# Three substitution groups with two rows a step, the outputs' norm on ScalarE, and a read result added by two engines

## What is computed

```python
h = tokens(x)                                   # 64 x 37 x 256
h = h + attention0(layernorm(h))                # 16 heads, shared keys and values
h = h + ffn0(layernorm(h))                      # entmax router, two factored layers
h = h + attn1(layernorm(h))
h = h + ffn1(layernorm(h))                      # 8 experts, the best one for each token

# attn1, for each image and each of 2 heads (d = 128), C = one chunk of up to 64 positions:
k = x / norm(x);  beta = sigmoid(x @ W_beta.T);  v = (x @ W_write.T) * beta
A0 = tril(-((k * beta) @ k.T) * L, -1)          # L: powers of the decay
A  = solve_triangular(eye - A0, eye)            # an inverse of a 37 x 37 unit triangle
o  = (tril(k @ k.T * L)) @ (A @ v)
out = x + o @ W_read.T
```

## Time and profile before

| | |
|---|---|
| median of 3 runs | 834.07 us (833.72 to 834.9) |
| the profiled execution | 836.92 us, span 835.1 us |
| mean granted clock of TensorE | 0.886 |
| PE busy | 678.3 us (81% of the span), 4562 matmuls |
| DVE busy | 448.1 us (54%), 1266 instructions |
| ACT busy | 229.1 us (27%) |
| POOL busy | 260.3 us (31%) |

### The profile page before, as it was taken

One profiled execution on the slowest core, in us unless ns is written; L12 is line 12 of the kernel. 1 busy time (PEld: TensorE's weight loads), 2 busy tenths in 40 slices (PEclk: granted clock), 3 DMA queues, 4 the chain that ended last, 5 costly groups with the idle time before them and its releaser, 6 DMA issues. The chain is left out here.

```text
span 835.1 us, 13690 instructions
## 1 busy us (share of the span) xinstructions
PE 678.3 (81%) x4562; PEld 519.5 (62%) x4562; DVE 448.1 (54%) x1266; ACT 229.1 (27%) x635; POOL 260.3 (31%) x418
## 2 busy tenths in 40 slices
PE   5899999999977149999983385196569999999994
PEld 4567677777755139999972364085436767667673
DVE  1567777777765742444799199466613333333321
ACT  0223333333322043443431022032013232232321
POOL 2344444444441012455453122022012221222211
PEclk9899999999986558999997589578569999999998
DMA  8211111111000000000100670193411111111110
GB/s 303 93 35 34 34 35 34 34 35 33 2 2 1 0 2 0 7 7 6 25 7 4 171 303 1 27 356 96 196 50 39 57 47 50 57 44 52 51 32 20
DMA packets 24643, 49.77 MB, mean 60 GB/s; under 512 B 15284, under 2 KB 15414, under 8 KB 23936
## 3 DMA queue, kind: packets, MB, share of 16 engines
q1 hardware_dynamic: 20960, 34.43, 12.7%
q0 software_dynamic: 3328, 10.23, 4.0%
q10 hardware_dynamic: 288, 4.25, 1.3%
HBM read 39.03 MB, written 9.86 MB: 59 GB/s over the span
## 5 line engine op out<-in xcount | busy, mean ns | idle before, releaser
L1762 PE MATMUL psum<-arena_w,work 128*128 x208 | 95.9, 605 | 1.0 <-DVE work L1814 1.0
L1860 ACT ACTIVATE work<-psum,cst 128x128 f32<-128x128 f32 x208 | 56.6, 383 | 144.1 <-PE psum L1775 144.1
L1786 PE MATMUL psum<-arena_w,work 128*128 x416 | 94.2, 379 | 0.4 <-ACT work L1860 0.4
L1786 PEld LDWEIGHTS psum<-arena_w,work 128*128 128x128 f32 x416 | 77.1, 190 | 10.5 <-issue 1.1
L1724 POOL DMA_INDIRECT out<-work,row_i x26 | 25.8, 990 | 160.2 <-DVE work L1836 160.2
L1823 DVE COPY work<-psum 128x512 f32<-128x512 f32 x52 | 36.0, 692 | 70.0 <-PE psum L1762 61.9
L346 PE MATMUL psum<-arena_w 128*111 128x256 f32 x264 | 64.1, 396 | 4.9 <-DMA arena_w<-in_pack 4.9
L1762 PEld LDWEIGHTS psum<-arena_w,work 128*128 128x128 f32 x208 | 38.3, 194 | 40.1 <-issue 40.1
L711 POOL TENSOR_TENSOR arena_w<-arena_w,work 101x592 f32<-101x592 f32 x33 | 39.6, 1200 | 72.2 <-DVE work L577 72.2
L346 PEld LDWEIGHTS psum<-arena_w 128*111 128x111 f32 x264 | 46.5, 183 | 19.7 <-issue 9.6
L1130 PE MATMUL psum<-tokens,work 111*111 111x128 f32 x88 | 18.2, 340 | 43.4 <-POOL work L1537 43.4
(11 more groups left out here) (216 smaller groups left out, 1344.6 us busy)
## 6 DMA issues: line engine op xcount, KB each, us to landing
arena_w<-in_w SPq DMA_DIRECT2D x2, 4096.0 KB, 13.3
arena_w<-in_x SPq DMA_DIRECT2D x22, 333.0 KB, 2.9
x_rows<-tokens SPq DMA_DIRECT2D x22, 192.0 KB, 5.7
arena_w<-in_pack ACTq DMA_DIRECT2D x1, 2420.0 KB, 10.9
cst<-in_packc ACTq DMA_DIRECT2D x1, 1727.0 KB, 14.9
arena_w<-in_pack SPq DMA_DIRECT2D x1, 818.5 KB, 7.3
arena_w<-in_pack SPq DMA_DIRECT2D x2, 384.0 KB, 4.6
work<-a_rows SPq DMA_DIRECT2D x21, 32.4 KB, 2.0
```

Of the source, the lines that this page charges most:

```text
L1762: mm = nc.tensor.matmul(bank[2 * j + f][:, :], xgt[j][:, k * 128:(k + 1) * 128], arena_w1[:, bass.ds(expert * (2 * FF) + (k * FF + f * 512 ...
L1786: mm = nc.tensor.matmul(bank[7][:, 0:D], ht[j][:, g * 128:(g + 1) * 128], arena_w2[:, bass.ds(expert * (FC * D) + g * D, D)], start=(g == ...
L1860: nc.scalar.activation(ht[j][:, g * 128:(g + 1) * 128], bank[4 + f][:, k * 128:(k + 1) * 128], ACT.Gelu, bias=cst[:, bass.ds(expert * FC + ...
```

## The change

1. Three groups: pairs 0 to 4 (60 systems), 5 to 7 (36) and 8 to 10 (32), with 2, 3 and 4 column sets on 120, 108 and 128 partitions. Each has its own place for systems and columns, so a load waits no longer for the group before. The unit columns are set by one comparison against a new constant `col_no`, ahead of the loop (the last group's at its end).
2. A step does two rows. Beforehand every second row of the system takes up the multiple of the row above it (`spare`, two passes over 18 x 36 elements), so that two rows can be found at once; the substitution has 18 steps and not 36, and each multiply and reduce covers two rows.
3. DVE's slots get budgets (0.7, 0.8, 4.2, 1.1). Unfinished groups stand in a queue; tile 0, 10 and 16 ask that groups 0, 1 and 2 be done. Nothing has to be finished ahead of the last pair.
4. `decay_products` masks both heads in one instruction, and the strengths are multiplied in by a third operation of POOL's `fold`.
5. SP stores and loads the inverses of group 0 after the systems of tile 18, ahead of those of tiles 19 to 21, loads the systems of the last group, then stores and loads the inverses of group 1, then loads W1.
6. In the tile loop ACT scales the first half of a read-out from PSUM (`scale_first`), POOL adds it to the row (`add_first`), and DVE adds the second half only. POOL computes the negated mean times the scale, and ACT does the norm. `add_read` comes one iteration later, turning and logits two.

```diff
-CUTS = [i if i < 8 else 6 if i < 18 else 16 for i in range(TOK)]
-GROUPS = ((0, 6), (6, PAIRS))
-SLOTS = (1.0, 1.0, 5.0, 1.7)
+GROUPS = ((0, 5), (5, 8), (8, PAIRS))
+SETS = [128 // (2 * (min(B, 6 * p1) - 6 * p0)) for p0, p1 in GROUPS]
+COLS = [-(-TOK // sets) for sets in SETS]
+SLOTS = (0.7, 0.8, 4.2, 1.1)
...
                 def load_systems(g):
                     im0, im1, nb, stride, sets = group_of(g)
                     stored = 2 * GROUPS[g][1]
+                    rows_n, _ = place_of(g)
                     for b in range(NB):
                         sp.wait_ge(n_stored[b], 16 * len(ROW_CUTS) * len(range(b, stored, NB)))
-                    sp.wait_ge(cleared, 1)
-                    if g:
-                        sp.wait_ge(solved[g - 1], 1)
+                    if g == LAST:
+                        sp.wait_ge(z1_done, PAIRS)
...
                 for g in range(len(GROUPS)):
                     for t in range(2 * GROUPS[g][0], 2 * GROUPS[g][1]):
                         store_systems(t)
-                    if g:
-                        store_inverses(g - 1)
+                        if t == NT - NB and g == LAST > 0:
+                            store_inverses(0)
+                            load_inverses(0)
                     load_systems(g)
-                for g in range(LAST):
+                for g in range(1, LAST):
+                    store_inverses(g)
                     load_inverses(g)
...
-                for t in range(NT + 3):
+                for t in range(NT + 5):
                     solve_values(t)
                     read_out(t - 1)
-                    turn_outputs(t - 3)
+                    turn_outputs(t - 5)
                     attend(t)
-                    router_logits(t - 3)
+                    router_logits(t - 5)
...
+                def scale_first(t):
+                    if not tile(t):
+                        return
+                    act.wait_ge(r_done, t + 1)
+                    act.wait_ge(inverted, t // 2 + 1)
+                    free(act, half_added, t - 1)
+                    nc.scalar.activation(first_half[t % 2], bank[4 + t % 2][0:R, 0:D], ACT.Copy,
+                                         scale=inv_all[:, t * H1:t * H1 + 1]).then_inc(half_out, 1)
+
+                def normalise_outputs(t):
+                    if not tile(t):
+                        return
+                    act.wait_ge(powered2, t + 1)
+                    nc.scalar.activation(x_half(t), h_rows(t), ACT.Identity, bias=ve2[t % 2][:, 2:3],
+                                         scale=ve2[t % 2][:, 1:2]).then_inc(normed2, 1)
...
-                for t in range(NT + 3):
+                for t in range(NT + 5):
+                    normalise_outputs(t - 4)
                     copy_solved(t)
-                    copy_turned(t - 3)
+                    copy_turned(t - 5)
+                    scale_first(t - 1)
                     copy_attended(t)
...
-                    dve.wait_ge(strong, t + 1)
                     free(dve, nk_ready, t - 1)
-                    for h in range(H1):
-                        cols = slice(h * R, (h + 1) * R)
-                        last = nc.vector.scalar_tensor_tensor(nf[t % 2][:, cols], bank[7][0:R, cols],
-                                                              strength[:, t * H1 + h:t * H1 + h + 1], ln[:, cols],
-                                                              ALU.mult, ALU.mult)
-                    last.then_inc(n_masked, 1)
+                    nc.vector.tensor_tensor(nf[t % 2], bank[7][0:R, 0:H1 * R], ln, ALU.mult).then_inc(n_masked, 1)
...
+                    dve.wait_ge(n_in[g], 16 * H1 * sets)
+                    for which in range(2):
+                        free(dve, chain[which], steps[which])
+                    links = rows_n[0:used, 2 * TOK + 1:TOK * TOK:2 * TOK + 2]
+                    nc.vector.tensor_tensor(spare, n[:, 1::2, 0:TOK - 1], links.unsqueeze(2).broadcast_to([used, half, TOK - 1]),
+                                            ALU.mult).then_inc(paired[g], 1)
+                    dve.wait_ge(paired[g], 1)
+                    nc.vector.tensor_tensor(n[:, 2::2, 0:TOK - 1], n[:, 2::2, 0:TOK - 1], spare, ALU.add).then_inc(paired[g], 1)
...
+                    yield 2.2
+                    for i in range(1, TOK, 2):
+                        most = (i + 1) // sets + 1
+                        parts = [(0, 0, min(split, most))]
+                        if split < most:
+                            parts.append((1, split, most))
...
-                            nc.vector.tensor_tensor(w, x[:, c0:c1, j0:end],
-                                                    n[:, i, j0:end].unsqueeze(1).broadcast_to([used, c1 - c0, end - j0]),
+                            nc.vector.tensor_tensor(w, x[:, c0:c1, j0:i + 2].unsqueeze(1).broadcast_to(shape),
+                                                    n[:, i:i + 2, j0:i + 2].unsqueeze(2).broadcast_to(shape),
                                                     ALU.mult).then_inc(chain[which], 1)
                             steps[which] += 1
-                            cost += 2 * (0.16 + (c1 - c0) * (end - j0) / 960)
+                            cost += 2 * (0.15 + 2 * shape[2] * shape[3] * 0.0012)
                         for (which, c0, c1), w in zip(parts, products):
                             dve.wait_ge(chain[which], steps[which])
-                            nc.vector.tensor_reduce(x[:, c0:c1, i], w, AX_X, ALU.add).then_inc(chain[which], 1)
+                            nc.vector.tensor_reduce(x[:, c0:c1, i:i + 2].rearrange("p c r -> p r c"), w, AX_X,
+                                                    ALU.add).then_inc(chain[which], 1)
...
-                    for k, mark in enumerate((half_added, added)):
-                        nc.vector.scalar_tensor_tensor(h, bank[4 + j][0:R, k * D:(k + 1) * D],
-                                                       inv_all[:, t * H1 + k:t * H1 + k + 1], h,
-                                                       ALU.mult, ALU.add).then_inc(mark, 1)
-                        dve.wait_ge(mark, t + 1)
+                    dve.wait_ge(half_added, t + 1)
+                    nc.vector.scalar_tensor_tensor(h, bank[4 + j][0:R, D:2 * D], inv_all[:, t * H1 + 1:t * H1 + 2], h,
+                                                   ALU.mult, ALU.add).then_inc(added, 1)
...
                     advance(SLOTS[0])
-                    if i - 2 in ends:
-                        advance(math.inf)
                     decay_products(i - 2, 0)
                     add_outputs(i - 1)
                     advance(SLOTS[1])
                     normalise(i - 1)
                     decay_products(i - 2, 1)
-                    if i - 2 not in ends:
-                        advance(SLOTS[2])
-                    elif ends[i - 2] < LAST:
-                        pending[0] = substitution(ends[i - 2])
-                advance(math.inf)
-                pending[0] = substitution(LAST)
-                firsts = [2 * p0 for p0, _ in GROUPS]
-                for t in range(NT + 3):
-                    if t == firsts[LAST]:
-                        advance(math.inf)
-                    normalise_outputs(t - 2)
-                    add_read(t - 1)
-                    keep_logits(t - 3)
+                    advance(SLOTS[2])
+                    if i == PAIRS:
+                        identity_columns(LAST)
+                    if i - 2 in ends:
+                        queue.append(substitution(ends[i - 2]))
+                firsts = {2 * p0: g for g, (p0, _) in enumerate(GROUPS)}
+                for t in range(NT + 5):
+                    if t in firsts:
+                        advance(math.inf, LAST - firsts[t])
+                    add_read(t - 2)
+                    keep_logits(t - 5)
                     if t > 0:
                         advance(SLOTS[3])
...
                     link(tt(to, parts[:, 0], parts[:, 1], ALU.add))
-                    tt(to, to, parts[:, 2], ALU.add).then_inc(nk_ready, 1)
+                    link(tt(to, to, parts[:, 2], ALU.add))
+                    tt(to, to, strength[:, t * H1:(t + 1) * H1].unsqueeze(2).broadcast_to([R, H1, TOK]),
+                       ALU.mult).then_inc(nk_ready, 1)
...
+                def add_first(t):
+                    if not tile(t):
+                        return
+                    pool.wait_ge(half_out, t + 1)
+                    pool.wait_ge(summed, t // 2 + 1)
+                    tt(h_rows(t), h_rows(t), first_half[t % 2], ALU.add).then_inc(half_added, 1)
+
+                for t in range(-2, NT + 2):
+                    power_outputs(t - 2)
+                    add_first(t - 1)
                     spread_inverses(t + 2)
```

128 lines of the change are left out of this document (62 added, 66 removed).

## The result

The changed kernel takes 807.18 us (median of 4 runs, 802.78 to 807.8), beside 834.49 us for the kernel before on the same chip: ratio 0.966, 95% interval 0.963 to 0.970. 804 had been predicted, with 794 to 815 as the range. The profiled execution took 807.8 us (span 806.0, mean granted clock of TensorE 0.903).

What follows compares the result with a forecast made beforehand. PE was taken to bound the pair loop, DVE the 12 tiles of group 0. An earlier last group (19.4 us) and its shorter part (10.8) sum to 30.2, off the median 834.07: 804 us, range 794 to 815.

Steps and rivals of the forecast that it cites:

- Substitution price: Substitution on DVE: 1.04 ns an element, 0.067 us an instruction; groups 23.2, 18.1 and 15.6 us, 57 in all.
- Rival (c): Substitution: two-row forms cost 2.08 ns an element, DVE's work grows by 33 us; 842 us; chance 0.04.
- Pair loop: DVE's waits for loaded systems, preparations and steps make the loop 7.6 us late by turn 11; bounds 2 to 12.
- One sign of being wrong: Pair loop: PE's clock falling within it was named among the signs that the forecast is wrong.
- Rival (b): Pair loop: loads land before they are asked for, so it loses 2 us, not 7.6; 798 us; chance 0.22.
- First tile: Tile loop's start: first product at 459.9, 13.7 us earlier; first add_read at 470.8 behind a load, so 8.2 arrive.
- Time per tile beside substitution: Tile loop, iterations 2 to 12: 2.9 us plus up to 0.4 for DVE steps meeting POOL's work, 3.3 us each.
- rival (a): Tile loop: POOL and DVE block each other, eleven iterations lose 0.62 us more each; 811, with clock 815; chance 0.19.
- Time per tile without it: Tile loop without substitution: 2.9 us a tile instead of 3.09, a gain of 0.2 us; PE's own work 2.75.
- The ring: Tile loop: DVE's add and statistics 1.44 us, POOL's power 0.55, second operation 0.27, add 0.62, a hop: 2.9.
- Last round: Last group: solved at 509.5, tile 16 starts at 521.2, 19.4 us earlier; its part takes 32.2 us, not 43.0.
- Rival (d): End of the block: 44 row stores on the SP queue at 0.71 us each end it; 807 to 811 us; chance 0.09.

Runs made afterwards that it cites:

- the run with POOL's other order: The changed kernel with POOL's add of a tile's first half put ahead of its power of the tile before: 798.03 us, ratio 0.955.
- the one with slot 1.6: The kernel with the three edits, five planned us of group 1's substitution ahead of the tile loop, and its slot 1.6 planned us, not 1.1: 785.19 us.
- the three edits: The changed kernel with substitution queued later in turns 7 and 10, no slot before the tile loop's fourth iteration, POOL's add ahead of its power: 793.99 us.

## Why the prediction was right, and where its steps were not

The median is 3 us above the forecast and inside its own range of 800 to 808. The block gave 26.8 us, where the sum had 30.2. That the number came so near is in part luck: group 2 was solved 6 us later than forecast, and a store's landing put 4 us too long took most of that back. Without that error the sum would have been near 800 (an estimate: 804 less 3.65), 7 us below the measured time.

- **Substitution price: right.** The last step of group 0 makes 2 x 1,054 element passes in 2.55 us; less four instructions at 0.067 that is 1.08 ns an element, beside the 1.04 taken. The preparation with its memset takes 1.93 us (390.99 to 392.92), 1.95 predicted. Rival (c) is out.
- **Pair loop: mechanism right, size wrong.** The term named was the landing of a load, 2 us by estimate. It took 3.65 us from the last issue (387.34) for group 0 and 3.3 for group 1. DVE waited 3.33 and 3.96 instead of 2.0 and 3.0. By turn 11 the loop was 12.0 us late (58.1 beside 46.1 for four turns of 11.70), not 7.6: turn 7 lost 5.5 us where the sum had 2.6, turn 9 2.0 for 1.1, turn 10 4.4 for 3.9. The run without the waits has 9.4 of the 12.0 for them and 2.6 for the rest; the sum had 6.5 and 1.1. Longer waits explain 1.3 us of turn 7 and 1.0 of turn 10 at most, the remainder stays open. One sign of being wrong did come: PE's clock fell within the pair loop. In the kernel after it was at 0.50, the 1.2 GHz level, behind PE's wait of 1.98 us in turn 7 (view of windows: length, busy us of PE, PEld, DVE, ACT and POOL, granted clock, DMA share, GB/s):

```profile
394.20:400.90 6.70, 6.70 (x20) 5.61 (x20) 6.24 (x22) 2.59 (x11) 4.19 (x11) 0.50 0.06 11
```

  Its price seems small. Turn 10 takes 16.07 us here, at full clock, and 16.13 in the run with POOL's other order, where the clock fell in that turn as well. In the run with the later queue, without the waits, the clock is 1.00 from 389 to 440. Rival (b), that loads land in time, is out; made true by moving the queue, it gave 802.5 and not 798, since part of what was moved turned up in the tile loop.
- **First tile: 5 us late**, 3.5 from the loop (the last mask) and the rest from POOL's folds behind it, which took 2.8 us and not 1.1. The first add_read did stand behind group 2's load, as predicted, but to move the add_reads ahead of this wait brought nothing at the end. The text counted 5.5 of the 13.7 us as lost there; the true limit of this stretch is the time at which group 2 is solved.
- **Time per tile beside substitution: 3.37 us measured, 3.3 predicted.** The number is right, its parts are not: 2.9 and up to 0.4 were predicted, 3.07 of ring and 0.28 of a longer power (see rival (a)) came.
- **Time per tile without it: the step that failed.** The ring was named with all its members and summed to 2.9; it is 3.07. The lengths of its rows fit (1.43, 0.55, 0.27 and 0.64), but the hand-overs come on top: 0.10 between the power and the second operation and 0.13 from POOL's add to DVE's. The second operation and the add overlap by 0.05. And "2.75 is PE's own" was read off as cycle minus idle; the run in the other order shows 2.58. So the prize for cutting the ring was 0.5 us a tile and not 0.15, and I passed over it. ScalarE's two operations take 0.48 and 0.62 us, not 0.37 each; here that stays hidden.
- **Last round: solved 6 us late, restarted only 2 us late.** Of the 6 us 2.3 are the signal that waits for a slot, a term that the sum did not have. The stores' landing was put at 5 us after the earlier trace rows, where four larger stores had it; here the load followed 1.35 us after the last issue (518.51 after 517.16). This is the error that cancelled. The cold clock after the hole and the drain were a little under-counted, 1.3 and 0.2 us.
- **Rival (a), POOL and DVE block each other**, is half true. Timeline of the kernel after, the power in an early slot and in a late one:

```profile
479.54 0.56 POOL L1568 TENSOR_TENSOR work<-work 111x1 f32<-111x1 f32 x1 [1.14 <-DVE work L1454]
...
509.71 0.79 DVE L1412 TENSOR_TENSOR work<-arena_w 128x296 f32<-128x296 f32 x2
509.80 1.11 POOL L1568 TENSOR_TENSOR work<-work 111x1 f32<-111x1 f32 x1 [1.04 <-DVE work L1454]
```

  The power of one element grows from 0.55 to 1.11 us with the size of the multiply that it meets (0.67, 0.80, 0.92, 1.02 between). But POOL's add of 0.64, which was to do the harm, falls where DVE is waiting for it, so the rival's 0.62 us a tile did not come. The power, though, is a member of the ring, and what it grew by, 0.28 us on average over the ten tiles, is nearly all of the difference between a tile beside substitution (3.37) and one without (3.07).
- **Rival (d), the SP queue**, does not decide in the kernel after, where the logits come last, if only by some 0.2 us. It does in the run with the old tile loop and in the one with slot 1.6, where 44 stores take 26.73 and 26.59 us: 0.61 us each, not 0.71.

## What to carry to other kernels

When work is moved to another engine, write the ring of waits that is left over all engines in their program order; if it closes within one iteration, first ask whether two steps of one engine can change places, since here that was worth 9 us and the move alone 2. An instruction that waits for a load should be queued where the load has landed by the trace, and what is moved out of a slot has to be given another one, or it appears as a hole at the next deadline. A wait is worth removing only if the next deadline moves with it: two add_reads taken from behind 9.85 us of waiting brought nothing, while 3.33 and 3.96 us of waiting, with the preparations behind them, cost nine in their loop and nearly five at the end.

## What the runs showed of the hardware

A DVE multiply with both inputs in SBUF and a POOL add of 512 elements did not run side by side. In the kernel with the three edits:

```profile
441.80 1.09 POOL L1515 TENSOR_TENSOR tokens<-tokens,arena_w 111x512 f32<-111x512 f32 x1
...
442.01 1.03 DVE L1412 TENSOR_TENSOR work<-arena_w 108x130 f32<-108x130 f32 x1
...
443.40 0.39 DVE L1412 TENSOR_TENSOR work<-arena_w 108x150 f32<-108x150 f32 x1
```

The multiply of 130 elements takes 1.03 us and ends 0.15 after the add; the next, with 150, takes 0.39. By the Trainium skill (SBUF — State Buffer, "Who interferes with whom") such a pair shuts each other out for a whole instruction; the trace agrees, and it shows it the other way round as well, in POOL's power above. What it costs depends on where the longer operation stands: POOL's add of a tile falls in DVE's wait and costs nothing, the power costs 0.28 us a tile.

With twelve stores issued within 8.2 us behind a transfer of 4,096 KB, the inverses' stores, issued 12 us after the last of them, took 5.4 us longer to land; the DMA share was 1.03 from 484 to 494.
